# Sixteen-head attention and windowed transformer kernel: one eviction moved from ScalarE to VectorE, and the planner's times of the windowed stage replaced

## The chip, the cores and the metric

One Trainium2 chip, one of its cores. The metric is the device time of one execution in microseconds (us); three executions of the kernel before gave 5361.24 to 5370.43 us, median 5363.51 us.

## The reference

Input x is 4 sequences of 1024 tokens with 128 features, fp32. Four residual parts follow each other, each on a normalised x:

```python
x = x + L0_attn(layernorm(x))     # A: 16 heads of 8, rotary, full softmax attention
x = x + L0_ffn(layernorm(x))      # B: 6 layers of windowed attention (16 heads of 64, window 32,
                                  #    l2-normalised rotary q and k) and a gated feed-forward net
x = x + L1_attn(layernorm(x))     # C: 16 heads of 8, rotary, causal attention
x = x + L1_ffn(layernorm(x))      # D: 4-head attention with shared k and v, then 8 experts, top 2
```

The part A and part C core, for each batch and head:

```python
scores = einsum('bhqd,bhkd->bhqk', q, k) / sqrt(8)
out = einsum('bhqk,bhkd->bhqd', softmax(scores), v) @ wo.T
```

## The kernel before

The four stages run one after the other with a meeting of all engines between them. In each stage one list of steps is made on the host (`order`), and each engine walks through the list and issues only its own part of every step. So the list fixes, engine by engine, a strict order; engines wait for each other by semaphores. A bank of PSUM has a pair of counters, filled and emptied.

**Stages A and C** (`mha_stage`) work on 16 units, each a batch and four heads, in slots. In a slot TensorE makes two score tiles of 128 queries x 512 keys ("first", L457), from which VectorE takes the row maxima (L638), and two score tiles of the transposed kind ("second", L473), of which ScalarE makes the exponentials (L569). The "first" of a unit run while the "second" of the unit before run. "first" has a ring of three banks (0 to 2), "second" and the transposes share a ring of four (3 to 6). Every two slots "values" (L486, eight matmuls) multiplies the exponentials by v and adds into bank 7; after eight of these (stage A; four or eight in the causal stage C) a chunk of 512 queries is done. The step "finish" then copies bank 7 to the tile ot (L577), so that the next chunk's "values" may begin, and "turn_back" transposes ot (L495) for VectorE to divide by the sums (L662, L669). "finish" sorts ahead of the "first" steps of its slot. There are 32 "finish" steps in each of the two stages. Once per batch, VectorE also does the layer norm of the batch to come, in three bursts ("norm").

**Stage B** (`local_stage`) handles 192 tiles (6 layers, 4 batches, 8 tiles of 128 tokens) as a software pipeline planned by `local_order`. Tile i has a due time for each step: PERIOD (15.8) times i plus the time in PIECES; the feed-forward steps of a batch take three places per period at the times in FF_PIECES ("fill" for TensorE, "empty" for the engine that reads the bank). The events are sorted by time; nothing but their order reaches the chip. Norm steps of a batch (20 small ones, L1221, L1224 and after) and "apply" steps (8, L1202) have fixed times of their own, and fall in one period of eight each. The steps of a tile, with their lines: "project" (L986, banks 0 and 1), "square" (ScalarE, L1133), "rope" (VectorE, L1263 and L1267), "sum_squares" (L1275), "add" (GpSimd, L1407, L1409), "invert" (ScalarE square root L1137, VectorE L1281, L1283), "scale" (GpSimd, L1416), "turn" (TensorE, L994, banks 2 and 3), "copy_turned" (ScalarE, L1149), "score" (L1009, L1030, banks 4 and 5), "top" (L1292), "less" (L1301), "exp" (ScalarE, L1155), "sum" (L1307), "invert_sum" (L1312), "weigh" (GpSimd, L1423), "block" (VectorE transpose, L1320), "gather" (L1047, banks 4 to 7), "spread" (ScalarE, L1163), "out" (L1062), "join" (L1329). The feed-forward steps use bank 6; their "empty" on VectorE is L1355 (0.70 us) or L1363 (0.25 us).

The lines that place a step:

```python
    def put(period, time, *step):
        events.append((PERIOD * period + time, len(events), step))
    ...
    for i, (l, b, t) in enumerate(stream):
        for kind, times in PIECES.items():
            for c, time in enumerate(times):
                put(i, time, kind, i, c)
    ...
    return [step for _, _, step in sorted(events)], stream, number
```

Of the kernel before, what the change touches and what calls it, by code (L numbers as in the profile page):

```python
# [23 lines left out]
BANK = 512  # L24
# [278 lines left out]
def mha_stage(chip, name, w_names, biases, rot, causal):  # L303
    nc, ins, x, ident, banks = chip.nc, chip.ins, chip.x, chip.ident, chip.banks
    filled, emptied = chip.filled, chip.emptied
    dim, scale = 8, float(1.0 / np.sqrt(np.float32(8)))
# [3 lines left out]
    number, slot = chip.place(order, dict(  # L310
        first=cycle((0, 1, 2)), **{kind: singles for kind in ("second", "weights", "turn_x", "project", "turn_k", "turn_q1",
                                                           "turn_q2", "turn_back", "turn_o", "conclude")}))
# [5 lines left out]
    end_of_values = {step[1:3]: step for step in order if step[0] == "values"}  # L318
# [3 lines left out]
    with ExitStack() as scope:  # L322
# [8 lines left out]
        top = sb("top", [TILES, HEADS_PER_UNIT])  # L331
# [184 lines left out]
        def scalar_():  # L516
            e, q = nc.scalar, chip.scalar
            for step in order:
# [43 lines left out]
                if kind == "second":  # L562
# [4 lines left out]
                    if j >= PROBS:  # L567
                        q.wait_ge(sem["valued"], number["values", *seconds[j - PROBS][1:4]])
                    e.activation(prob[j % PROBS][:, lo:BANK], banks[n][:, lo:BANK], ACT.Exp,  # L569
                                 scale=scale).then_inc(emptied[n], 1)  # L570
                if kind == "finish":
                    c = step[2]
                    q.wait_ge(sem["valued"], number[end_of_values[i, c]])
                    if i:
                        at, turned = slot["turn_back", i - 1, c]
                        q.wait_ge(filled[at], turned)
                    e.copy(ot[:, BANK * c:BANK * (c + 1)], banks[7]).then_inc(sem["finished"], 1)  # L577
                if kind == "turn_o":
                    c = step[2]
                    q.wait_ge(filled[n], use)  # L580
# [5 lines left out]
        def vector_():  # L586
# [22 lines left out]
            for step in order:  # L609
# [30 lines left out]
                if kind == "shift":  # L640
                    mine = slice(4 * (i % 4), 4 * (i % 4) + 4)
                    high, low = (qx[i // 4 % 2][:, :, mine, 3 * dim + m] for m in range(2))
                    for back in range(3):
                        at, reduced = slot[firsts[number[end_of_first[i]] - 1 - back]]
                        q.wait_ge(emptied[at], reduced)
                    q.wait_ge(sem["zeroed"], i // 4)
                    e.tensor_reduce(top[:, :, :], top2[i % 2][:, :, :, :].rearrange("p t c g -> p t g c"), AX.X, ALU.max,
                                    negate=True).then_inc(*chain.step())
                    q.wait_ge(*chain.now())
                    at, turned = slot["turn_q1", i, CHUNKS - 1]  # L650
                    q.wait_ge(filled[at], turned)
                    e.tensor_copy(high, top[:, :, :]).then_inc(*chain.step())
                    q.wait_ge(*chain.now())
                    e.tensor_tensor(low, top[:, :, :], high.bitcast(F32), ALU.subtract).then_inc(sem["shifted"], 1)
                if kind == "turn_back":
                    c = step[2]
                    of_heads = banks[n].rearrange("p (t g w) -> p t g w", t=TPB, g=HEADS_PER_UNIT)
                    q.wait_ge(filled[n], use)
                    if number[step] > 1:
                        at, evicted = slot[("turn_back", i, 0) if c else ("turn_back", i - 1, CHUNKS - 1)]  # L660
                        q.wait_ge(emptied[at], evicted)
                    e.reciprocal(rsum[:, :, :], of_heads[:, :, :, dim]).then_inc(*chain.step())  # L662
                    q.wait_ge(*chain.now())
                    if i >= 4:
                        at, turned = slot["turn_o", i // 4 - 1, CHUNKS - 1]
                        q.wait_ge(filled[at], turned)
                    to = o[:, TPB * c:TPB * (c + 1), (i % 4) * 32:(i % 4 + 1) * 32].rearrange(
                        "p t (g d) -> p t g d", g=HEADS_PER_UNIT)
                    e.tensor_tensor(to, of_heads[:, :, :, 0:dim], bcast(rsum[:, :, :], 3, dim),  # L669
                                    ALU.mult).then_inc(emptied[n], 1)  # L670
# [79 lines left out]
NORM_BEGINS, NORM_STEP, APPLY_BEGINS, APPLY_STEP, BIAS_BEGINS = 2.0, 0.55, 2.0, 0.6, 6.0  # L750
MOVE_X, PLACE_X, MOVE_F, PLACE_F, SHIFT_CUT = 5.0, 12.0, 7.0, 16.5, 112
PIECES = dict(
    project=(0.29, 2.26, 8.62, 12.22), square=(3.47, 8.24, 10.89, 13.29), rope=(4.23, 10.44, 11.24, 15.80),
    sum_squares=(9.15, 11.10, 12.42, 15.72), add=(12.15, 16.43, 18.41, 19.63), invert=(14.25, 15.94, 16.10),
    scale=(18.56, 19.37, 19.62, 27.79), turn=(18.81, 20.62, 23.32, 29.42), copy_turned=(20.83, 23.54, 26.19, 30.02),
    score=(30.62, 32.29), top=(34.55, 34.71), less=(35.28, 35.71), exp=(35.59, 36.09),
    sum=(36.29, 36.51), invert_sum=(36.39, 37.10), weigh=(36.53, 37.46), block=(37.59, 39.49),
    gather=(43.67,), spread=(42.51, 42.52, 43.74, 47.20), out=(49.64, 51.29, 52.13, 52.87), join=(54.63,))
INVERT_PARTS = len(PIECES["invert"])
NORM_ROOT = 2 * TILES + 1  # L760
FF_PIECES = dict(fill=(15.99, 20.10, 24.25), empty=(17.52, 21.35, 24.51))
def local_order():


# [1400 lines left out]
```

## Time and profile before

| | |
|---|---|
| median of three runs | 5363.51 us (5361.24 to 5370.43) |
| the profiled execution | 5370.43 us, span 5369.1 us |
| TensorE / VectorE / ScalarE / GpSimd busy | 92% / 82% / 68% / 54% |
| stage A, about | 60 to 850 us |
| stage B, about | 900 to 3980 us |
| stage C, about | 4100 to 4700 us |
| stage D, about | 4760 to 5369 us |

The profile is of one execution, the slowest of the three, so its time stands 6.9 us above the median. A busy share of TensorE counts from the start of a matmul to its modelled end, so that neighbouring matmuls overlap in it. The column PEclk is the granted TensorE clock, 1.00 for 2.4 GHz and 0.50 for 1.2 GHz. In a timeline a row joins like instructions that follow each other; in brackets stands the idle time of the engine before it and the engine, tile and line that ended it.

### The profile page before, as it was taken

The page shows a single profiled execution, that of the slowest core. Times are in us where ns is not written, and L with a number is a line of the kernel's source. Part 1 is how long each engine was busy: PE and PEld are TensorE (multiplying, and loading weights), DVE is VectorE, ACT ScalarE, POOL GpSimd, SP SyncE. Part 2 cuts the span into 40 slices and gives each one's busy share as a digit, 9 for nine tenths or more (in the row PEclk, how much of TensorE's full clock was granted, in tenths as well). Part 3 has the DMA queues.
Part 4 walks back from the last instruction along what each step waited for, and adds up shares of the span by engine and source line. Part 5 has one row for each costly group of instructions (what it writes and reads, how often), then busy time and mean ns, then how long its engine had stood idle before and what let it go on. Part 6 is the DMA issues. An engine that isn't in the chain of part 4 may idle for free. (4 is left out here: it accounts for less than half of the span.)

```text
span 5369.1 us, 142691 instructions
## 1 busy us (share of the span) xinstructions
PE 4948.3 (92%) x59480; PEld 2999.0 (56%) x59480; DVE 4396.4 (82%) x9191; ACT 3628.2 (68%) x6463; POOL 2880.2 (54%) x3367
## 2 busy tenths in 40 slices
PE   6999997999999999999999999999986999978978
PEld 2333333666666666666666666666654555544445
DVE  7998995988898888989898989899945777567665
ACT  2888885777777777777777777777742777645522
POOL 2121003878777877787778777877731111024624
PEclk6999998999999999999999999999985999888989
DMA  0000002000000000000000000000000000000000
GB/s 23 1 1 1 1 1 71 14 10 10 26 14 10 10 25 14 10 10 26 14 10 10 27 16 12 10 10 14 4 3 24 2 2 2 2 15 1 1 1 16
DMA packets 46742, 63.25 MB, mean 12 GB/s; under 512 B 11261, under 2 KB 33603, under 8 KB 45203
## 3 DMA queue, kind: packets, MB, share of 16 engines
q1 hardware_dynamic: 46098, 54.14, 3.4%
q8 instruction: 469, 7.68, 0.6%
q14 instruction: 175, 1.43, 0.1%
HBM read 25.17 MB, written 4.19 MB: 5 GB/s over the span
## 5 line engine op out<-in xcount | busy, mean ns | idle before, releaser
L1062 PE MATMUL psum<-b_w_vo,b_mixed 128*128 128x128 f32 x6144 | 828.1, 278 | 3.4 <-ACT b_mixed L1163 3.2
L986 PE MATMUL psum<-b_w_qk,b_xst 128*128 128x512 f32 x1536 | 810.1, 609 | 9.2 <-DVE b_cross L1267 8.1
L1416 POOL TENSOR_TENSOR x<-x,b_norm 128x512 f32<-128x512 f32 x576 | 588.3, 1042 | 374.8 <-DVE b_norm L1283 374.8
L1062 PEld LDWEIGHTS psum<-b_w_vo,b_mixed 128*128 128x128 f32 x6144 | 751.9, 192 | 66.9 <-issue 50.0
L638 DVE TENSOR_REDUCE a_top<-psum 128x1 f32<-128x512 f32 x1024 | 637.4, 682 | 77.7 <-PE psum L457 75.8
L569 ACT ACTIVATE a_prob<-psum 128x512 f32<-128x512 f32 x1024 | 557.0, 606 | 117.7 <-PE psum L473 107.5
L1133 ACT ACTIVATE x<-psum 128x512 f32<-128x512 f32 x768 | 465.3, 606 | 204.6 <-DVE b_norm L1275 191.4
L1163 ACT COPY b_mixed<-psum 128x512 f32<-128x512 f32 x768 | 411.0, 587 | 230.7 <-PE psum L1047 230.7
L1275 DVE TENSOR_REDUCE b_norm<-x 128x8 f32<-128x512 f32 x768 | 513.9, 672 | 61.6 <-ACT x L1133 58.6
L1267 DVE TENSOR_TENSOR b_cross<-psum,b_table 128x512 f32<-128x512 f32 x768 | 521.3, 679 | 0.0
L638 DVE TENSOR_REDUCE c_top<-psum 128x1 f32<-128x512 f32 (+3 forms) x768 | 383.5, 551 | 151.9 <-PE psum L457 149.2
L1407 POOL TENSOR_TENSOR x<-x,b_cross 128x256 f32<-128x256 f32 x576 | 418.6, 727 | 147.5 <-DVE b_cross L1267 146.2
L1423 POOL TENSOR_TENSOR b_prob<-b_prob,b_stat 128x512 f32<-128x512 f32 x384 | 394.7, 1049 | 130.0 <-DVE b_stat L1312 126.3
L569 ACT ACTIVATE c_prob<-psum 128x512 f32<-128x512 f32 (+3 forms) x768 | 334.9, 501 | 152.7 <-PE psum L473 148.4
L1409 POOL TENSOR_TENSOR x<-x,b_cross 128x256 f32<-128x256 f32 x576 | 419.4, 728 | 0.0
L457 PE MATMUL psum<-a_kt,a_q 32*128 32x512 f32 x1024 | 358.7, 528 | 63.2 <-DVE a_top L638 57.3
L1263 DVE TENSOR_TENSOR x<-psum,b_table 128x512 f32<-128x512 f32 x576 | 390.8, 678 | 18.5 <-ACT x L1133 17.7
L1030 PEld LDWEIGHTS psum<-b_k_t,b_q_t 64*32 64x32 f32 x26368 | 308.2, 105 | 161.9 <-issue 131.1
L986 PEld LDWEIGHTS psum<-b_w_qk,b_xst 128*128 128x128 f32 x1536 | 246.6, 191 | 250.5 <-DVE b_cross L1267 138.3
L457 PEld LDWEIGHTS psum<-a_kt,a_q 32*128 32x128 f32 x1024 | 148.3, 193 | 389.7 <-DVE a_top L638 308.7
L994 PEld LDWEIGHTS psum<-ident,x 128*128 128x128 f32 x2304 | 278.2, 141 | 156.8 <-issue 132.2
L1030 PE MATMUL psum<-b_k_t,b_q_t 64*32 64x64 f32 (+1 forms) x26368 | 346.1, 220 | 2.9 <-issue 2.7
(326 smaller groups left out, 11042.7 us busy)
## 6 DMA issues: line engine op xcount, KB each, us to landing
b_prev<-b_xs_x SPq DMA_DIRECT2D x24, 384.0 KB, 3.5
b_w_qk<-in_L_ffn_Wqkv SPq DMA_DIRECT2D x6, 1024.0 KB, 7.1
b_shifted_x<-y SPq DMA_DIRECT2D x24, 224.0 KB, 2.5
b_shifted_f<-y SPq DMA_DIRECT2D x24, 224.0 KB, 2.5
b_w_v<-in_L_ffn_Wqkv SPq DMA_DIRECT2D x6, 512.0 KB, 7.4
b_w_o<-in_L_ffn_Wo SPq DMA_DIRECT2D x6, 512.0 KB, 9.2
b_prev<-b_xs_x SPq DMA_DIRECT2D x24, 112.0 KB, 3.3
x<-in_L_attn_x SPq DMA_DIRECT2D x4, 512.0 KB, 6.8
```

The lines of the kernel that those rows point to most:

```text
L457: e.matmul(banks[n][:, 0:wide], q1[i % 2][part, P * t:P * (t + 1)], kt[i % 3][part, BANK * c:hi], start=not corner, stop=True, skip_group_ ...
L569: e.activation(prob[j % PROBS][:, lo:BANK], banks[n][:, lo:BANK], ACT.Exp, scale=scale).then_inc(emptied[n], 1)
L638: e.tensor_reduce(top2[i % 2][:, t, c, head:head + 1], banks[n][:, 0:wide], AX.X, ALU.max).then_inc(emptied[n], 1)
L986: e.matmul(banks[n], xst_of(l, b)[:, P * t:P * (t + 1)], w_qk[l % 2][:, BANK * c:BANK * (c + 1)], start=True, stop=True).then_inc(filled[n ...
L1030: made = e.matmul(heads[rows, p, to, :], qt[half, p, rows], k[:, lo:lo + wide].rearrange("p (s q) -> p s q", q=WINDOW), start=False, stop= ...
L1062: made = e.matmul(banks[n][:, 0:D], mixed[:, h, :], w_vo[l % 2][:, h, :], start=h == 0, stop=h == 2 * PAIRS - 1)
L1133: e.activation(square[r % 2], banks[n], ACT.Square).then_inc(sem["squared"], 1)
L1267: e.tensor_tensor(by_head(cross[(nth[step] - 1) % 3]), by_head(banks[n]), bcast(table[:, t, k + 1, :], 1, HPC), ALU.mult).then_inc(emptied ...
L1275: e.tensor_reduce(norm[i % 2][:, 0, HPC * c:HPC * (c + 1)], by_head(square[r % 2]), AX.X, ALU.add).then_inc(sem["summed"], 1)
L1407: e.tensor_tensor(rh[:, :, 0:half], rh[:, :, 0:half], xh[:, :, half:LDIM], ALU.subtract).then_inc(*chain.step())
L1409: e.tensor_tensor(rh[:, :, half:LDIM], rh[:, :, half:LDIM], xh[:, :, 0:half], ALU.add).then_inc(sem["roped"], 1)
L1416: e.tensor_tensor(rh, rh, bcast(norm[i % 2][:, 1, HPC * c:HPC * (c + 1)], 2, LDIM), ALU.mult).then_inc(sem["scaled"], 1)
```

## The change

In stages A and C the copy of "finish" moves from ScalarE's walk through the list to VectorE's; its waits and its place in the list stay. In stage B all of PIECES but "rope" 0 and 1 and some further single values, and FF_PIECES, get other numbers. PERIOD, the norm, apply, move and place times stay.

```diff
@@ scalar_() of mha_stage
-                if kind == "finish":
-                    c = step[2]
-                    q.wait_ge(sem["valued"], number[end_of_values[i, c]])
-                    if i:
-                        at, turned = slot["turn_back", i - 1, c]
-                        q.wait_ge(filled[at], turned)
-                    e.copy(ot[:, BANK * c:BANK * (c + 1)], banks[7]).then_inc(sem["finished"], 1)
@@ vector_() of mha_stage
+                if kind == "finish":
+                    c = step[2]
+                    q.wait_ge(sem["valued"], number[end_of_values[i, c]])
+                    if i:
+                        at, turned = slot["turn_back", i - 1, c]
+                        q.wait_ge(filled[at], turned)
+                    e.tensor_copy(ot[:, BANK * c:BANK * (c + 1)], banks[7]).then_inc(sem["finished"], 1)
@@ PIECES
-    project=(0.29, 2.26, 8.62, 12.22), square=(3.47, 8.24, 10.89, 13.29), rope=(4.23, 10.44, 11.24, 15.80),
-    sum_squares=(9.15, 11.10, 12.42, 15.72), add=(12.15, 16.43, 18.41, 19.63), invert=(14.25, 15.94, 16.10),
-    scale=(18.56, 19.37, 19.62, 27.79), turn=(18.81, 20.62, 23.32, 29.42), copy_turned=(20.83, 23.54, 26.19, 30.02),
-    score=(30.62, 32.29), top=(34.55, 34.71), less=(35.28, 35.71), exp=(35.59, 36.09),
-    sum=(36.29, 36.51), invert_sum=(36.39, 37.10), weigh=(36.53, 37.46), block=(37.59, 39.49),
-    gather=(43.67,), spread=(42.51, 42.52, 43.74, 47.20), out=(49.64, 51.29, 52.13, 52.87), join=(54.63,))
+    project=(-0.02, 2.74, 8.92, 11.78), square=(2.41, 7.84, 10.76, 12.81), rope=(4.23, 10.44, 11.41, 15.62),
+    sum_squares=(9.27, 11.10, 12.03, 15.20), add=(12.65, 13.99, 17.94, 20.17), invert=(14.94, 17.16, 17.32),
+    scale=(19.10, 19.10, 20.57, 26.31), turn=(18.96, 22.74, 24.33, 29.08), copy_turned=(20.83, 22.40, 26.53, 30.10),
+    score=(30.19, 33.37), top=(33.89, 34.97), less=(34.99, 35.74), exp=(34.06, 36.34),
+    sum=(36.07, 36.88), invert_sum=(36.27, 36.99), weigh=(36.51, 36.91), block=(37.82, 40.61),
+    gather=(42.91,), spread=(42.72, 42.49, 43.36, 47.43), out=(49.27, 50.84, 52.64, 53.00), join=(56.06,))
-FF_PIECES = dict(fill=(15.99, 20.10, 24.25), empty=(17.52, 21.35, 24.51))
+FF_PIECES = dict(fill=(14.63, 20.66, 24.59), empty=(16.52, 21.90, 24.93))
```

## Rows read from the trace of the kernel before

**Rows 1.** The page: busy time and share of the span, by engine.
```profile
PE 4948.3 (92%) x59480; PEld 2999.0 (56%) x59480; DVE 4396.4 (82%) x9191; ACT 3628.2 (68%) x6463; POOL 2880.2 (54%) x3367
```

**Rows 2.** Busy time by stretch: stretch and length, engines, PEclk, DMA share, GB/s.
```profile
60.00:850.00 790.00, 728.37 (x4739) 277.33 (x4738) 666.87 (x1220) 618.91 (x1186) 97.66 (x54) 0.93 0.00 1
...
900.00:3900.00 3000.00, 2910.37 (x42974) 1970.37 (x42974) 2700.41 (x5483) 2242.39 (x3714) 2344.54 (x2913) 1.00 0.05 14
...
4100.00:4700.00 600.00, 574.02 (x7583) 317.72 (x7582) 415.87 (x951) 402.47 (x910) 70.38 (x48) 0.89 0.01 2
```

**Rows 3.** The same view, three stretches of stage A, the last two with a norm.
```profile
148.00:257.00 109.00, 100.42 (x711) 37.20 (x711) 101.61 (x181) 92.86 (x178) 8.75 (x6) 1.00 0.00 1
257.00:289.00 32.00, 28.81 (x171) 11.07 (x167) 27.54 (x69) 22.13 (x44) 0.00 (x0) 0.84 0.00 1
...
445.00:479.00 34.00, 32.59 (x168) 11.62 (x164) 27.55 (x69) 22.07 (x44) 0.00 (x0) 0.70 0.01 1
```

**Rows 4.** Line L577: min/median/max ns, first and last start; who waited for it.
```profile
L577 ACT COPY a_ot<-psum x32: 585/603/647, 147.0 to 845.7; 128x512 f32<-128x512 f32 x32
...
  PEld psum L486: 3.3, 13
```

**Rows 5.** Line L1334 of stage B: VectorE's copies of a full bank.
```profile
L1334 DVE COPY b_w_v<-psum x12: 652/684/692, 878.8 to 3105.4; 128x512 f32<-128x512 f32 x12
```

**Rows 6.** Waits of stage A, 60 to 850 us: waiter <- releaser: us, times, longest.
```profile
DVE a_rsum L662 <- PE psum L495: 42.3, 3, 16.5
```

**Rows 7.** Timeline of stage A around one "finish" (start, us, engine, line).
```profile
613.67 0.63 ACT L577 COPY a_ot<-psum 128x512 f32<-128x512 f32 x1
...
613.91 2.48 DVE L638 TENSOR_REDUCE a_top<-psum 128x1 f32<-128x512 f32 x4 [0.23 <-PE psum L457]
...
614.65 0.50 PE L457 MATMUL psum<-a_kt,a_q 32*128 32x512 f32 x1 [0.43 <-DVE a_top L638]
...
616.09 0.50 PE L457 MATMUL psum<-a_kt,a_q 32*128 32x512 f32 x2
...
616.62 1.29 DVE L638 TENSOR_REDUCE a_top<-psum 128x1 f32<-128x512 f32 x2 [0.23 <-PE psum L457]
```

**Rows 8.** Timeline of stage C around one "finish".
```profile
4192.48 3.38 DVE L638 TENSOR_REDUCE c_top<-psum 128x1 f32<-128x256 f32 x6 [0.46 <-PE psum L457]
...
4194.13 0.49 PE L457 MATMUL psum<-c_kt,c_q 32*128 32x512 f32 x1 [0.34 <-DVE c_top L638]
...
4196.18 1.02 DVE L638 TENSOR_REDUCE c_top<-psum 128x1 f32<-128x384 f32 x2 [0.31 <-PE psum L457]
```

**Rows 9.** Waits in stage B, 1000 to 3900 us.
```profile
POOL b_prob L1423 <- DVE b_stat L1312: 114.6, 120, 2.8
...
PEld psum L1047 <- DVE b_prob_t L1320: 113.1, 107, 1.8
...
DVE b_prob_t L1320 <- POOL b_prob L1423: 61.6, 138, 1.3
```

**Rows 10.** Timeline of a period of stage B with "apply" steps.
```profile
2343.15 1.26 ACT L1202 ACTIVATE b_xs_f<-b_xs_f,spread 128x128 f32<-128x128 f32 x3
...
2344.14 0.23 DVE L1363 TENSOR_TENSOR y<-y,psum 128x128 f32<-128x128 f32 x1
...
2346.31 1.04 POOL L1416 TENSOR_TENSOR b_rot<-b_rot,b_norm 128x512 f32<-128x512 f32 x1
...
2346.59 0.63 ACT L1155 ACTIVATE b_prob<-b_prob 128x512 f32<-128x512 f32 x1
...
2347.52 0.61 ACT L1155 ACTIVATE b_prob<-b_prob 128x512 f32<-128x512 f32 x1
...
2350.11 0.60 PE L994 MATMUL psum<-ident,b_rot 128*128 128x128 f32 x4
...
2350.89 0.71 DVE L1320 STREAM_TRANSPOSE b_prob_t<-b_prob 128x512 f32<-128x512 f32 x1 [1.17 <-POOL b_prob L1423]
```

**Rows 11.** Timeline of a period of stage B with norm steps, VectorE.
```profile
2335.61 0.21 DVE L1224 BATCH_NORM_AGGREGATE mean_var<-moments 128x2 f32<-128x6 f32 x2
```

## The prediction

> **What bounds the kernel now.** The page comes first: TensorE is busy for 92% of the span, VectorE for 82% [rows 1], so two engines are near their limit and the stages have to be read one by one. The view by stretches [rows 2] gives, of each 100 us: stage A 92 on TensorE and 84 on VectorE, stage B 97 and 90, stage C 96 and 69. ScalarE has 22 to 33% to spare in all three. In the steady part of stage A VectorE is busy for 93% [rows 3].
>
> The timeline shows what holds stage A [rows 7]. A round is two slots: four row maxima on VectorE, 2.48 us together and 0.60 us from one start to the next, then 0.23 us in which it waits for TensorE, and the round comes again after 2.71 us (613.91 to 616.62). It is a circle. The first maximum of a round frees a bank, for which the fourth "first" matmul waits (0.43 us at 614.65); behind it in TensorE's order stand two "second" matmuls and the eight "values" matmuls, which end about 616.09, then come the next "first" and the next maximum. So what makes the first maximum of a round late by some time makes everything late by that time. ScalarE's copy L577 isn't in the circle: the weight loads behind it waited 3.3 us in 13 cases of both stages [rows 4], and the round that holds a copy (613.67) takes the usual 2.71 us.
>
> In stage C VectorE has room on the average, but not at the end of a chunk [rows 8]: six maxima follow without a gap, and TensorE waits for the third of its banks at 4194.13. In stage B TensorE is the bound, with one wait that comes back in most tiles: the gather's weights wait for VectorE's transpose L1320, 113.1 us in 107 cases [rows 9]. It closes the circle of a tile: scores, top, less, exp, sum, weigh, block, gather, spread, and the next scores in the banks that spread has freed.
>
> **Part 1: the copy in stage A.** ScalarE loses 32 copies of 0.603 us [rows 4]; that gains nothing, since nobody waits for it. VectorE gets 32. It has no such copy in this stage; the nearest row is its copy of a full bank in stage B, 0.684 us [rows 5], and by the maxima such a thing takes 0.60 us of the engine from start to start [rows 7]. "finish" stands in VectorE's list ahead of the "first" of its slot, so the copy lands just where VectorE waits 0.23 us. The "values" it waits for have ended by then (ScalarE could start at 613.67, the four maxima before end there too). The first maximum starts 0.60 - 0.23 = 0.37 us later, the fourth "first" waits 0.80 us instead of 0.43, and nothing in the round takes that back. Three copies at the end lie where VectorE waits for TensorE anyway, 42.3 us in 3 cases [rows 6], and cost nothing. Two lie in the bursts of norms, where VectorE has no gap: 0.60 us each. Sum: 27 x 0.37 + 2 x 0.60 = 11.2 us. Bounds: 0, if TensorE made it up from the idle time of its own, and 29 x 0.68 = 20 us.
>
> VectorE sits farther from PSUM than ScalarE: the Trainium skill (Perfetto Trace Analysis, Optimizing Scalar/DVE Operations) gives about 125 ns of access overhead for the one and 51 ns for the other, and advises to offload a saturated VectorE to ScalarE, the reverse of this edit. The rows agree on the size, 0.684 against 0.603 us [rows 4, 5]; 74 ns on 64 copies would be an estimated 5 us of engine time.
>
> **Part 2: the copy in stage C.** 32 copies again, three of them in the tail. At a chunk end like that of [rows 8] the copy delays the maxima by 0.60 us, TensorE's wait of 0.34 us grows by it, and TensorE, 96% busy, has nothing to catch up with. At the other chunk ends the bank is only just free in time. I take 0.35 us, between nothing and 0.60: 29 x 0.35 = 10.2 us; bounds 0 and 29 x 0.68 = 20 us.
>
> **Part 3: the planned times.** Only the order counts, so I sort the times modulo 15.8 with both sets. In a usual tile just four things change places; the times move by up to 3 us, but mostly in company.
> - TensorE: "out" group 3 now runs before "turn" 1 (all but the first tiles). The turned piece is copied by ScalarE one such group later; ScalarE is 75% busy [rows 2], and the scores that need it are due 11 later in the new times (turn 1 22.74, score 1 33.37). 0.
> - ScalarE: "spread" 1 before "spread" 0. The four parts of a gather run side by side on four row groups of the array and end together. 0.
> - GpSimd: "add" 3 before "scale" 2, so scale 2 ends 1.5 us later. In [rows 10] it ends at 2347.35 and turn 2 starts at 2350.11: covered by 1.3 us. 0.
> - VectorE: the first "empty" of a period before the two "invert" steps, where VectorE does it (89 tiles: 44 of 0.23 us like that at 2344.14 [rows 10], 45 of 0.70). The inverse comes later by this, and so does scale 0 on GpSimd. GpSimd waits ahead of "weigh" in 120 tiles [rows 9], there it is swallowed. Taking 23 tiles (the "apply" ones, where GpSimd runs from scale to weigh without a stop) at 0.2 us: +4.6 us. Bounds 0 and 89 x 0.25 = 22 us.
>
> Two periods in eight also see the small steps, whose times stay, in another place. In the 23 "apply" periods exp 0 now goes ahead of four of the eight apply steps, which then stand between exp 0 and exp 1. Exp 0 can start earlier than the 2346.59 of [rows 10] by the apply step it passes, 0.4 us; four apply steps at 0.42 us (1.26 us for three) bring exp 1 to about 2348.5, 1.0 us later than 2347.52. VectorE's sum 1 waits for some 0.4 us, and block 0, which now waits 1.17 us for weigh, takes most of it: +0.1 us, 2.3 us in all; bounds -0.4 x 23 = -9 and +1.0 x 23 = 23 us. In the 23 norm periods two aggregations more go ahead of block 1, 0.2 us [rows 11]; but top 0, less 0 and the first sum each pass a norm step of about that size. I set these against each other, -0.1 us each, -2.3 us; bounds -6 and +5. Stage B: 4.6 + 2.3 - 2.3 = 4.6 us, rounded to +4, since a few of these overlap.
>
> **Sum.** 11.2 + 10.2 + 4 = 25.4 us. On the profiled execution's own 5370.4 us that makes 5395.8; the median of the runs shown is 6.9 us lower, so I say 5388.9, rounded to 5389 us.
>
> **The rivals.**
> - *The new order shortens the circle of stage B.* The place is the wait of gather for block. If scale, add and weigh on GpSimd mesh better and the softmax chain starts earlier, and that takes 0.35 us from each of the 107 waits of about 1.06 us [rows 9], then 37 us go: 5389 - 4 - 37 = 5348, faster than before. It decides once it is worth more than 32 us, 0.17 us for each of the 192 tiles. For it: that all tiles share this circle. Against it: the steps in the circle keep their places in the usual tile; only 46 periods see a change in it.
> - *The copies are hidden.* If the gap of VectorE and TensorE's own spare time take in the copies in both stages, only stage B's 4 us stay: 5368 us, no change. For it: VectorE's 31% of idle time in stage C. Against it: the circle of [rows 7], with 0.23 us of room.
> - *The clock falls more often.* In the two norm stretches of stage A the granted clock is 0.84 and 0.70 of 2.4 GHz [rows 3], that is 10 and 20 us at 1.2 GHz; VectorE's work is the same (27.54 and 27.55 us), the stretch is 2 us longer, so 10 us of the lower clock cost 2 us. A copy within each burst makes TensorE pause longer. Should six batch changes of A and C each lose 10 us more of full clock, that is 12 us: 5401 us. What the Trainium skill says (TensorE: Matmul & The Clock Gate, What's actually happening), that idleness brings the lower clock back and activity lifts it, agrees with these rows.
>
> **How the numbers follow.** Forecast 0.52, shorter circle 0.14, copies hidden 0.16, clock 0.12, others (stage B slower by more than its price, towards 5410) 0.06. Within 0.2% means 10.7 us on either side of 5363.5, about what a measurement of this kernel can tell from no change. Faster: the shorter circle and a little of the others, 0.15. Same: the hidden copies and the low end of the forecast, 0.20. Slower: 0.65. The forecast's own bounds, 5374 to 5402, come from the copies at half and at full price. The range leaves out the far half of the shorter circle and the worst of stage B: 5352 to 5404 us.
>
> **What the new profile would show.** Step 1: L577's work as a VectorE copy of 0.65 to 0.70 us; the round with a copy 3.08 us instead of 2.71; 148 to 812 us of stage A longer by about 10 us; ScalarE's busy time lower by 39 us and VectorE's higher by 44. Step 2: in stage C a longer wait of TensorE for the maxima L638. Step 3: stage B, first project to last, the same within 10 us, with the gather's wait for L1320 near its 113 us. The prediction is wrong if stage B moves by more than 20 us either way, which I can't exclude by a sorted list alone, or if rounds with a copy stay at 2.71 us.

## The result and the profile after

The changed kernel takes 5413.6 us (median of 5 runs, 5405.5 to 5421.6), the kernel before in the same series 5370.4 us. The ratio is 1.0079, with a 95% interval of 1.0058 to 1.0099: 43 us slower. The forecast was 5389 us with a range up to 5404; the sign was right, the size was not. The profiled execution after took 5425.4 us, with a span of 5424.1 us.

Busy time in the page of the changed kernel, which answers to [rows 1]:

```profile
PE 4975.2 (92%) x59480; PEld 3004.8 (55%) x59480; DVE 4434.1 (82%) x9255; ACT 3599.4 (66%) x6399; POOL 2883.1 (53%) x3367
```

VectorE has 64 instructions and 37.7 us more, ScalarE 64 fewer and 28.8 us less. These numbers say that the copies moved; they say nothing of where 43 us went. The same three stretches as in [rows 2] (stretch and length, busy time of PE, PEld, DVE, ACT, POOL, PEclk, DMA share, GB/s):

```profile
60.00:850.00 790.00, 721.80 (x4675) 273.31 (x4679) 682.13 (x1249) 600.65 (x1142) 97.58 (x54) 0.92 0.00 1
900.00:3900.00 3000.00, 2891.32 (x42486) 1949.79 (x42487) 2679.97 (x5445) 2213.60 (x3672) 2322.09 (x2885) 1.00 0.05 14
4100.00:4700.00 600.00, 560.43 (x7205) 315.75 (x7203) 434.76 (x988) 371.06 (x820) 74.18 (x50) 0.87 0.01 2
```

In the 3000 us of stage B all engines have done less: 42,486 matmuls instead of 42,974, at a granted clock of 1.00 in both. So stage B, in which nothing but an order changed, has become slower too. To compare stages I measure them in each trace between two marks of their own: A and C from the first to the last "turn_back" (L495) of the stage, B from the first matmul of "out" of its first tile to that of its last (191 tile periods).

| | A | B | C |
|---|---|---|---|
| before | 696.4 | 3037.3 | 545.4 |
| after | 706.9 | 3058.8 | 563.4 |
| difference | +10.5 | +21.5 | +18.0 |
| forecast | +11.2 | +4 | +10.2 |

The rest of the 55 us between the two profiled executions lies in the first and last tiles of B (2.5 us), in D (2.8 us, from its first matmul to the end) and between the stages. The largest error is in stage B. The waits of the forecast's circle there, 1000 to 3900 us, as in [rows 9]:

```profile
POOL b_prob L1423 <- DVE b_stat L1312: 98.6, 108, 2.6
...
PEld psum L1047 <- DVE b_prob_t L1320: 117.9, 110, 2.0
...
DVE b_prob_t L1320 <- POOL b_prob L1423: 62.2, 132, 1.4
```

The gather's wait has grown by 4.8 us and GpSimd's has shrunk by 16. The circle has neither shortened nor become the place of the loss. By the measure that the forecast named for stage B, first "project" to last, it is 23.3 us longer.

### The profile page after: what moved, and what is told of

The parts are those of the page before. It is cut to its first block and busy times, and to the rows that moved or that the text cites. A ratio compares the mean times of both kernels' runs of the same rounds, so it can differ in the third digit from the quotient of the medians.

```text
span 5424.1 us, 142815 instructions
## 1 busy us (share of the span) xinstructions
PE 4975.2 (92%) x59480; PEld 3004.8 (55%) x59480; DVE 4434.1 (82%) x9255; ACT 3599.4 (66%) x6399; POOL 2883.1 (53%) x3367
## 3 DMA queue, kind: packets, MB, share of 16 engines
q14 instruction: 176, 1.44, 0.1%
## 5 line engine op out<-in xcount | busy, mean ns | idle before, releaser
L986 PE MATMUL psum<-b_w_qk,b_xst 128*128 128x512 f32 x1536 | 811.4, 610 | 7.6 <-DVE b_cross L1267 6.4
L1062 PE MATMUL psum<-b_w_vo,b_mixed 128*128 128x128 f32 x6144 | 797.1, 278 | 3.2 <-ACT b_mixed L1163 2.9
L1062 PEld LDWEIGHTS psum<-b_w_vo,b_mixed 128*128 128x128 f32 x6144 | 736.9, 192 | 67.3 <-issue 50.6
L1030 PEld LDWEIGHTS psum<-b_k_t,b_q_t 64*32 64x32 f32 x26368 | 308.8, 105 | 172.5 <-issue 141.9
L1149 ACT COPY b_q_t<-psum 128x512 f32<-128x512 f32 x384 | 220.5, 574 | 263.5 <-PE psum L994 263.5
L986 PEld LDWEIGHTS psum<-b_w_qk,b_xst 128*128 128x128 f32 x1536 | 247.2, 191 | 249.6 <-DVE b_cross L1267 134.8
```

Of the source, the lines that this page charges most:

```text
L986: e.matmul(banks[n], xst_of(l, b)[:, P * t:P * (t + 1)], w_qk[l % 2][:, BANK * c:BANK * (c + 1)], start=True, stop=True).then_inc(filled[n ...
L1062: made = e.matmul(banks[n][:, 0:D], mixed[:, h, :], w_vo[l % 2][:, h, :], start=h == 0, stop=h == 2 * PAIRS - 1)
```

## The experiments

Each kernel below is the kernel before or after with one edit. A "pause" is a gap of more than 0.1 us between the starts of two neighbouring matmuls of one score burst (L1030, 26,368 matmuls in stage B); it is counted in the trace. Stage lengths and pauses are those of one profiled execution, medians and ratios those of 4 to 12 runs against 21 to 31 runs of the kernel before (for the changed kernel 5 against 5).

| kernel | median us | ratio (95%) | A | B | C | pauses, us |
|---|---|---|---|---|---|---|
| before | 5370.4 | | 696.4 | 3037.3 | 545.4 | 13, 5.2 |
| after | 5413.6 | 1.0079 (1.0058 to 1.0099) | 706.9 | 3058.8 | 563.4 | 34, 17.5 |
| e1 copy only | 5388.8 | 1.0035 (1.0019 to 1.0051) | 706.9 | 3037.8 | 555.2 | 12, 5.6 |
| e2 times only | 5388.3 | 1.0034 (1.0023 to 1.0045) | 698.0 | 3059.5 | 538.6 | 33, 17.3 |
| e3 out 3, turn 1 | 5368.1 | 0.9997 (0.9984 to 1.0009) | 698.0 | 3043.4 | 556.6 | 14, 8.6 |
| e4 empty, invert | 5371.1 | 1.0001 (0.9988 to 1.0013) | 698.8 | 3040.5 | 538.6 | 19, 7.4 |
| e5 apply places | 5372.5 | 0.9995 (0.9980 to 1.0011) | 698.1 | 3038.9 | 557.2 | 14, 6.6 |
| e6 norm places | 5369.7 | 0.9997 (0.9984 to 1.0009) | 697.9 | 3042.3 | 538.6 | 13, 6.0 |
| e7 add 3 and spread 1 | 5382.5 | 1.0029 (1.0013 to 1.0045) | 698.7 | 3054.2 | 535.2 | 35, 19.6 |
| e8 table later | 5362.2 | 0.9990 (0.9975 to 1.0006) | 698.1 | 3035.4 | 556.7 | 16, 7.8 |
| e9 add 3 only | 5375.3 | 1.0004 (0.9995 to 1.0014) | 697.8 | 3037.7 | 542.2 | 14, 6.5 |
| e10 spread 1 only | 5387.9 | 1.0027 (1.0016 to 1.0039) | 697.8 | 3049.7 | 548.8 | 33, 13.7 |
| e11 after, both back | 5404.5 | 1.0062 (1.0049 to 1.0075) | 703.6 | 3046.6 | 561.0 | 9, 6.8 |
| e12 table later, again | 5361.0 | 0.9984 (0.9976 to 0.9993) | 698.7 | 3034.3 | 545.5 | 16, 7.2 |
| e13 spread 1 and masks | 5374.1 | 1.0015 (1.0003 to 1.0026) | 698.2 | 3043.3 | 538.7 | 12, 6.8 |
| e14 masks only | 5371.4 | 1.0002 (0.9991 to 1.0014) | 698.1 | 3043.7 | 548.9 | 26, 12.0 |
| e15 after and masks | 5412.4 | 1.0086 (1.0066 to 1.0106) | 704.0 | 3049.2 | 559.0 | 13, 6.0 |
| e16 copy twice | 5537.8 | 1.0335 (1.0307 to 1.0363) | 767.7 | 3038.2 | 631.4 | 12, 5.3 |

Stage B repeats well: before, e1 and e16, which have the same order there, lie within 0.9 us. Stage C does not: with the same code it is 535 to 557 us long in 13 of these profiles. Differences of B can be read from single profiles, those of C only from several.

Time and granted clock go together: over the 110 executions of the kernel before, 0.001 of the mean clock goes with 3.5 us (correlation -0.93). Take the 244 executions of e1 to e15 and of the kernel before that ran beside them to equal clock by a straight line, each within its own series. Then the kernels stand above the kernel before by an estimated 14.8 us (e1), 20.0 (e2), 1.0 (e3), 2.6 (e4), 0.8 (e5), 3.2 (e6), 14.6 (e7), -7.3 (e8), 1.8 (e9), 12.4 (e10), 24.0 (e11), -4.5 (e12), 5.7 (e13), 7.0 (e14) and 27.1 (e15), each +-2 us, e11 and e15 +-3; the changed kernel, by the same line, about 34. What an edit costs by way of a lower clock isn't in these numbers. They bear out the lengths of B from single profiles, with one exception: e3, +6.1 us in its profile and 1.0 here.

**e1 and e2, the two halves of the change.**

```diff
 e1: "finish" in vector_() as after; PIECES and FF_PIECES as before
 e2: "finish" in scalar_() as before; PIECES and FF_PIECES as after
```

> The copy on VectorE alone, all planned times as before. Theory 1 (the copy sits in the circle of stages A and C): first to last transpose of the chunks in stage A longer by 10 to 11 us, in stage C by about 9 us plus what a stretch at the lower clock adds, stage B's 3037.3 us from the first to the last tile's first out group unchanged; time about 20 us above before. Theory 2 (the cost of the whole change lies in stage B only, C's 18 us were a chance stretch of the lower clock): about 11 us above before, C within 5 us.

> The new planned times alone, the copy on ScalarE as before. Theory 1 (the new order costs stage B about 21 us by fixed waits): stage B longer by 20 to 23 us, A and C as before, time 20 to 25 us above before. Theory 2 (pauses inside TensorE's score matmuls, 17 us in the profile after against 5 us before, are chance of one execution): stage B longer by some 10 us only.

The halves give 18.4 and 17.9 us of medians, 36 of the 43 us, and the intervals leave room for the rest; at equal clock they are 14.8 and 20.0 of about 34. In both, the first theory came true. The copy lengthens A and C and leaves B alone, the times lengthen B and leave A and C alone. The pauses came again in e2, 33 of them, so they are no chance of one execution.

**e3 to e7, the new order in parts.** Together their order changes are those of the new times, and no more.

```diff
 e3
-turn=(18.81, 20.62,
+turn=(18.81, 21.30,
 e4
-invert=(14.25, 15.94, 16.10)
+invert=(14.25, 17.60, 17.62)
 e5
-square=(3.47,
+square=(2.41,
-exp=(35.59, 36.09)
+exp=(34.06, 36.34)
 e6
-top=(34.55, 34.71), less=(35.28, 35.71)
+top=(33.89, 34.97), less=(34.99, 35.74)
-sum=(36.29, 36.51), invert_sum=(36.39, 37.10)
+sum=(36.07, 36.88), invert_sum=(36.27, 36.99)
-block=(37.59, 39.49), join=(54.63,), sum_squares=(9.15,
+block=(37.82, 40.61), join=(56.06,), sum_squares=(9.27,
-empty=(17.52, 21.35, 24.51)
+empty=(17.52, 21.90, 24.93)
 e7
-add=(12.15, 16.43, 18.41, 19.63), spread=(42.51, 42.52,
+add=(12.15, 16.43, 18.41, 19.50), spread=(42.51, 42.50,
```

> Before, with one place changed: out group 3 ahead of turn 1 on TensorE in 190 tiles. Theory 1 (the loss is in waits on GpSimd and ScalarE): stage B within 3 us of 3037.3, pauses inside the score matmuls near 5 us. Theory 2 (this swap brings the pauses inside the score matmuls): stage B 10 to 12 us longer, with pauses of about 17 us.

> Before, with one place changed: the first empty of a period ahead of the inverts on VectorE in 89 tiles. Theory 1 (scale 0 starts later, and where table steps keep GpSimd busy until weigh the delay goes through to the gather): stage B 5 to 8 us longer, most of it in the fourth batch of each layer, about 0.45 us in a tile with an empty of 0.65 us. Theory 2 (GpSimd's idle time ahead of weigh swallows it): within 2 us.

> Before, with square 0 and exp 0 ahead of the apply steps on ScalarE as in the change (23 tiles). Theory 1 (exp 1 comes 0.8 to 1 us later and VectorE's block waits): stage B 3 to 6 us longer, in the apply tiles. Theory 2 (block's wait for weigh swallows it): within 1 us.

> Before, with the steps of VectorE placed among the norm steps as in the change (23 tiles). Theory 1 (two aggregations ahead of block 1 delay the gather, nothing gives it back): stage B 3 to 4 us longer, in the norm tiles. Theory 2 (top, less and the first sum come earlier and pay for it): within 1 us or shorter.

> Before, with add 3 ahead of scale 2 on GpSimd and spread 1 ahead of spread 0 on ScalarE in all 192 tiles. Theory 1 (both are covered): stage B within 2 us of 3037.3. Theory 2 (the irregular losses of up to 0.6 us in single tiles come from scale 2 arriving late at turn 2, or from the spreads): 5 us or more longer.

Only e7 moves the median. Of the 22.2 us that e2 adds to stage B, e7 alone gives 16.9. The other four give 6.1, 3.2, 1.6 and 5.0 us in B, each below what their medians can tell from nothing; together with e7 that is more than e2, so they overlap. In e7 the second theory came true. The 5.0 us of e6 are above both of its theories and nearer to the first; e3, e4 and e5 lie between their two theories and decide nothing.

**e8 and e12, a side path.** Not part of the change: GpSimd's table steps are planned 1.9 us later.

```diff
-            put(i, max(PIECES["add"]) + 0.5, "table", l + 1, t)
+            put(i, max(PIECES["add"]) + 2.4, "table", l + 1, t)
```

> Not a part of the change: before, with the table steps (GpSimd, four operations of 0.33 us, 40 tiles) placed behind weigh 1 instead of ahead of weigh 0. Theory 1 (in the fourth batch of a layer GpSimd's chain from scale to weigh is what block waits for): stage B 10 to 20 us shorter, in those 40 tiles. Theory 2 (another wait takes its place at once): within 4 us.

> The kernel before with GpSimd's table steps planned 1.9 us later in the tile, as run once before in fewer rounds (5362.2 us against 5370.8, ratio 0.999 with an interval of 0.9975 to 1.0006). If the steps stood in the way of add and scale in the eight tiles of the table, the gain is some 2 us in stage B (3035.4 against 3037.3) and the ratio stays within 0.2% of 1: nothing that can be told from no change. Rival: the 8 us seen are real, ratio 0.9985 with an interval below 1.

The second series puts it 8.7 us under the kernel before, with an interval of 0.9976 to 0.9993. Stage B is 1.9 and 3.0 us shorter, so the gain of 10 to 20 us there, the first theory of e8, did not come. Of all kernels here it is the fastest, by 0.16%, which is real by its interval but less than the 0.2% named in the prediction, and where the rest of the 8.7 us comes from stays open.

**e9 and e10, e7 taken apart.**

```diff
 e9
-add=(12.15, 16.43, 18.41, 19.63)
+add=(12.15, 16.43, 18.41, 19.50)
 e10
-spread=(42.51, 42.52,
+spread=(42.51, 42.50,
```

> The kernel before with one swap only: GpSimd's add 3 ahead of its scale 2 (planned time of add 3 from 19.63 to 19.50). Together with the swap of spread 1 and spread 0 it lengthened stage B (first to last tile of out 0) by 16.9 us (3054.2 against 3037.3) and the time by 12 us, with 35 pauses of over 0.1 us inside the score matmuls, 19.6 us together, where the kernel before has 13 and 5.2 us. Theory add: GpSimd's order sets when the instruction blocks of TensorE are fetched; this kernel alone shows stage B at 3054 +-4 us, 30 or more pauses, a median near 5382 us. Theory spread: ScalarE's order does it; then stage B is 3037 to 3042 us here, 12 to 19 pauses, 5370 us. Theory both: about 3046 us.

> The kernel before with one swap only: ScalarE's spread 1 ahead of its spread 0 (planned time of spread 1 from 42.52 to 42.50). Theory add: nothing comes of it, stage B 3037 to 3042 us, 12 to 19 pauses in the scores, 5370 us. Theory spread: stage B 3054 +-4 us, 30 or more pauses, 5382 us. Theory that any small shift of the schedule reshuffles the pauses by chance: both halves differ from the kernel before, and the two do not add up to 16.9 us.

It is the swap on ScalarE: B +12.4 us with "spread" 1 first, +0.4 with "add" 3 first. (The two add up to 12.8, e7 had 16.9 in its one profile. At equal clock they are 1.8 and 12.4 us, e7 14.6, so nothing is left over that the executions show.) What happens is seen in tile 146, which starts at 3258.89 us in the kernel before and at 3271.46 in e10. The timeline of the kernel before, TensorE and ScalarE:

```profile
3268.75 0.30 PEld L986 LDWEIGHTS psum<-b_w_qk,b_xst 128*128 128x128 f32 x2 [0.76 <-DVE b_cross L1267]
...
3268.81 1.56 ACT L1163 COPY b_mixed<-psum 128x512 f32<-128x512 f32 x3 [1.21 <-PE psum L1047]
...
3272.69 0.86 PE L1030 MATMUL psum<-b_k_t,b_q_t 64*32 64x64 f32 x64
...
3273.48 0.71 PE L1062 MATMUL psum<-b_w_vo,b_mixed 128*128 128x128 f32 x4
```

And that of e10:

```profile
3281.23 0.30 PEld L986 LDWEIGHTS psum<-b_w_qk,b_xst 128*128 128x128 f32 x2 [0.76 <-DVE b_cross L1267]
...
3281.34 1.56 ACT L1163 COPY b_mixed<-psum 128x512 f32<-128x512 f32 x3 [1.24 <-PE psum L1047]
...
3285.17 0.43 PE L1030 MATMUL psum<-b_k_t,b_q_t 64*32 64x64 f32 x25
...
3286.13 0.64 PE L1030 MATMUL psum<-b_k_t,b_q_t 64*32 64x64 f32 x39 [0.53 <-issue]
...
3286.70 1.16 PE L1062 MATMUL psum<-b_w_vo,b_mixed 128*128 128x128 f32 x8
```

Two things are to be seen. The three copies begin 0.11 us after L986's weights, not 0.06: the part that is now copied first is ready later, by 0.04 us in the median of the tiles. And score 1, one burst of 64 matmuls before, breaks off after 25 and goes on 0.53 us later. No engine is named as the releaser, only "issue": TensorE had no instructions. All 33 pauses of e10 lie, to within four matmuls, a whole number of blocks of 126.5 matmuls apart. Such a block is one packet of 16,384 bytes on the DMA queue of kind "instruction": there are 469 packets for the 118,960 weight loads and matmuls and 1,266 semaphore instructions, 256 for each packet. In tile 146 the packet that matters starts 10.28 us after the tile's start in the kernel before and at 12.12 in e10, and takes 1.3 us; until then TensorE's rows agree to 0.01 us. The pause ends at 14.78, 1.4 us after the packet is in.

The same holds of every pause. In the 17 kernels of the table without e16 there are 326 pauses. Ahead of each of them the last instruction packet is the one that belongs to this place of the program, counted from the start, and the pause ends 1.2 to 1.7 us after this packet is in. So the pauses are waits for instructions, and they begin where a packet comes too late for the burst.

The Trainium skill (Runtime: NRT & Kernel Launch, Instruction fetch mechanics) describes just such blocks of 16 KiB that the sequencer fetches by itself while it executes the one before, and holds the cost of a boundary to be mostly hidden. The trace of the kernel before agrees in the main, with 13 pauses and 5.2 us; in e10 (33 pauses, 13.7 us) and in the changed kernel (34, 17.5 us) much less of it is hidden.

**e11, the two swaps undone in the changed kernel.**

```diff
-add=(12.65, 13.99, 17.94, 20.17), spread=(42.72, 42.49,
+add=(12.65, 13.99, 17.94, 20.60), spread=(42.48, 42.49,
-            put(i, max(PIECES["add"]) + 0.5, "table", l + 1, t)
+            put(i, max(PIECES["add"]) + 0.07, "table", l + 1, t)
```

> The changed kernel with these two swaps undone (scale 2 ahead of add 3, spread 0 ahead of spread 1; the table steps stay in their place), all other new orders and the copy on VectorE kept. If the two swaps carry the loss of stage B in the changed kernel as they do alone, stage B comes to 3040 to 3048 us instead of 3058.8, the pauses in the scores to about 7 us instead of 17.5, and the median to 5413.6 - 15 = about 5399 us, with ratio 1.005. Rival: the pauses belong to the sum of the new orders, and undoing two of them leaves stage B at 3055 to 3060 us and the median at 5410 to 5415 us.

Stage B gets 12.2 us shorter and the pauses go down to 9. The ratio to the kernel before falls from 1.0079 to 1.0062; the two intervals overlap, so the stage says it more surely than the time. At equal clock it is 24.0 us instead of about 34.

**e13 to e15, why a swap on ScalarE starves TensorE.** The scores of the next tile go into banks 4 and 5, which "spread" 0 and 1 empty. Ahead of score 0 TensorE makes its masks (L1009), four into bank 4 and four into bank 5, each four behind a wait for their bank. These kernels turn that order round.

```diff
-                    for odd in range(2 if step[2] == 0 else 0):
+                    for odd in ((1, 0) if step[2] == 0 else ()):
```

> The kernel before with spread 1 ahead of spread 0 on ScalarE (which alone gave stage B 3049.7 us instead of 3037.3 and 33 pauses inside the score matmuls, 13.7 us together) and with TensorE's masks for score 0 taking bank 5 ahead of bank 4 too. Theory late release: TensorE's sequencer stands at the wait for bank 4 ahead of the masks; with spread 1 first, bank 4 is copied 0.48 us later, the sequencer runs through the block of instructions 0.5 us later, the next block is fetched 0.5 us later, and score 1 catches up with it. Taking bank 5 first gives the lead back: stage B 3037 to 3040 us, 12 to 19 pauses of 5 to 8 us, median 5370 us. Rival, the order on ScalarE itself (its copies start 0.04 us later in each tile): stage B stays at 3048 to 3051 us with 30 or more pauses, median 5387 us.

> The mirror of it: the kernel before, spread 0 first as it was, but the masks for score 0 take bank 5 ahead of bank 4. Theory late release: TensorE now waits first for the bank that is copied second, so this costs what the swap of the spreads costs: stage B 3048 to 3052 us, 30 or more pauses of 13 us or more, median about 5385 us. Rival, the order on ScalarE itself: nothing changes, 3037 to 3040 us, 5370 us.

> The changed kernel with one more edit: the masks for score 0 take bank 5, which its spread 1 now frees first, ahead of bank 4. Theory late release: as with the two swaps undone (stage B 3046.6 us instead of 3058.8, 9 pauses of 6.9 us): stage B 3045 to 3049 us, median about 5402 us, ratio 1.006. Rival: 3057 to 3060 us and 5412 us.

The four kernels make a square:

| | masks: bank 4 first | masks: bank 5 first |
|---|---|---|
| spread 0 copied first | before: 3037.3 us, 13 pauses | e14: 3043.7 us, 26 pauses |
| spread 1 copied first | e10: 3049.7 us, 33 pauses | e13: 3043.3 us, 12 pauses |

Wherever TensorE first asks for the bank that is copied second, the pauses double; where both orders agree, they are as few as in the kernel before, whichever bank leads. The trace shows each step between. TensorE's sequencer records the wait ahead of the masks as an instruction of its own. It ends 0.7 us after the start of the first copy in 160 of 190 tiles in the kernel before, e13 and e15, and 1.2 us after it in the same number in e10, e14 and the changed kernel: one copy later. In the other 30 another wait comes first. Behind it the sequencer runs on through its program, ahead of the array (in tile 146 of the kernel before the wait ends 0.76 us before the first mask), and with it the fetching. Of 79 packets that the kernel before requests between 11.3 and 13.5 us of a tile, those that come over 0.3 us later are 35 in e10 and 32 in e14, but 7 in e13, and 9 in e1 and in e9; 41 in the changed kernel, 11 in e15. The waits of TensorE in the scores for "issue", 900 to 3900 us (total, times, longest), one fence each for the kernel before, e14, e10, e13, after and e15:

```profile
PE psum L1030 <- issue: 2.7, 3, 1.8
```

```profile
PE psum L1030 <- issue: 6.8, 12, 1.9
```

```profile
PE psum L1030 <- issue: 6.6, 14, 2.0
```

```profile
PE psum L1030 <- issue: 4.2, 2, 2.2
```

```profile
PE psum L1030 <- issue: 9.7, 23, 1.5
```

```profile
PE psum L1030 <- issue: 3.0, 5, 1.9
```

This is only the part that lies behind a row's last modelled end, but the times fall into the same two groups. The square also adds up: the mismatch alone costs 6.4 us (e14), the order of the copies alone 6.0 us (e13), both 12.4 (e10). My expectation for e13 and e14 missed this: I had put all 12.4 us on the mismatch. At equal clock it is 7.0 us for e14, 5.7 for e13 and 12.4 for e10, from 11 or 12 executions each, though the median of e14 shows nothing. Of the 6.0 us of e13, 3.5 lie in 64 periods that are 0.02 to 0.1 us longer, which fits copies that start 0.04 us later: the kernels with "spread" 1 first have 48 to 64 such periods, those with "spread" 0 first 7 to 15. The other 2.5 us are in larger, irregular differences, and neither part was tried by itself. In e15 stage B came down by 9.6 us, as expected, but the median of its four runs, 5412.4 us, did not; at equal clock it is 27.1 us instead of about 34.

**e16, the copy made twice.**

```diff
-                    e.tensor_copy(ot[:, BANK * c:BANK * (c + 1)], banks[7]).then_inc(sem["finished"], 1)
+                    e.tensor_copy(ot[:, BANK * c:BANK * (c + 1)], banks[7]).then_inc(*chain.step())
+                    q.wait_ge(*chain.now())
+                    e.tensor_copy(ot[:, BANK * c:BANK * (c + 1)], banks[7]).then_inc(sem["finished"], 1)
```

> The kernel before with the copy on VectorE, and made twice, the second after the end of the first (0.68 us and some 0.05 us of waiting). The same values are written twice. With one copy stage A grew by 10.5 us and stage C by 9.8 us. If the copy lies in a circle without room, as the prediction has it, all of the second copy is added: stage A 706.9 + 29 x 0.73 = 728 us, +-3; stage C 555 + up to 21 = 565 to 576 us; stage B stays at 3037.8; the median about 5388.8 + 40 = 5425 to 5430 us. Rival, a loss that comes from a changed order of events and not from VectorE's time: stage A stays below 715 us.

Against the kernel with one copy A grew by 60.8 us and C by 76.2, where 21 and at most 21 were expected; both theories missed it. In the chunks that go undisturbed the addition is as expected: 23.26 us instead of 22.54, +0.72. The others show another thing, here in a round of stage A of e16:

```profile
560.76 0.69 DVE L656 COPY a_ot<-psum 128x512 f32<-128x512 f32 x1
...
561.36 2.48 DVE L631 TENSOR_REDUCE a_top<-psum 128x1 f32<-128x512 f32 x4
562.10 0.79 PE L457 MATMUL psum<-a_kt,a_q 32*128 32x512 f32 x1 [1.44 <-DVE a_top L631]
...
565.52 1.29 DVE L631 TENSOR_REDUCE a_top<-psum 128x1 f32<-128x512 f32 x2 [1.68 <-PE psum L457]
```

TensorE stood still for 1.44 us, and its next "first" takes 0.79 us instead of 0.50: the granted clock has fallen to 1.2 GHz, and now VectorE waits 1.68 us for TensorE. Over 148 to 812 us the mean granted clock is 0.89 here and 0.98 in the kernel before. In stage A one copy per chunk costs its own time, and a second one costs the clock as well; in stage C the first one already does.

## Why the prediction was wrong, step by step

**What bounds the kernel** was read rightly for A and C. For B the bound was right (TensorE), but the list of what can stop it was not: it held waits for data and banks, not TensorE's own supply of instructions.

**Part 1, stage A: the mechanism was right, its size too high by half.** Against the kernel before it is 10.5 us after and in e1, with 11.2 predicted. But that profile of the kernel before happens to be the shortest in A. The 13 kernels with the old copy have a mean of 698.1 us there, and the four with the new one (706.9 twice, 703.6, 704.0) of 705.4: 7.3 us, with the same time at 1.2 GHz (35 and 36 us). VectorE's copy was given 0.65 to 0.70 us and measured:

```profile
L654 DVE COPY a_ot<-psum x32: 678/679/692, 147.3 to 856.6; 128x512 f32<-128x512 f32 x32
```

A round with the copy, in the timeline after, beside [rows 7]:

```profile
620.27 2.48 DVE L631 TENSOR_REDUCE a_top<-psum 128x1 f32<-128x512 f32 x4 [0.22 <-PE psum L457]
...
622.67 0.68 DVE L654 COPY a_ot<-psum 128x512 f32<-128x512 f32 x1
...
623.26 2.47 DVE L631 TENSOR_REDUCE a_top<-psum 128x1 f32<-128x512 f32 x4
624.00 0.49 PE L457 MATMUL psum<-a_kt,a_q 32*128 32x512 f32 x1 [0.70 <-DVE a_top L631]
...
625.97 1.29 DVE L631 TENSOR_REDUCE a_top<-psum 128x1 f32<-128x512 f32 x2 [0.23 <-PE psum L457]
```

The copy does land ahead of the first maximum, VectorE's wait is gone, and the fourth "first" waits longer. But it waits 0.70 us, not 0.80, and from 620.27 the next round begins after 2.99 us, not 3.08. The step was mis-sized: I subtracted the idle time of 0.23, which counts from the end of the last maximum, from a price of 0.60 that counts from start to start. From start to start four maxima take 2.40 of 2.71 us, so 0.31 us is free, and 0.60 - 0.31 = 0.29. The chunks without a norm grew by about 0.3 us each. Around the two bursts of norms, priced at 0.60 us each, the means of the four kernels are 1.2 us longer in the first and 0.1 us shorter in the second. The last three chunks, priced at nothing, took 0.5 us less. The busy times, forecast at 39 us less on ScalarE and 44 more on VectorE, came to 28.8 and 37.7. They count overlapping instructions once, so the price is again the one from start to start: 64 x 0.60 = 38 us on VectorE, and on ScalarE, where three copies take 1.56 us and so 0.48 each, 64 x 0.48 = 31.

**Part 2, stage C: the mechanism was right, but half of the cost is the clock's.** e1 had +9.8 us for the predicted 10.2. At an undisturbed chunk end like that of [rows 8], in e1, the same stretch takes 4.05 us instead of 3.70, the 0.35 us that I took:

```profile
4238.48 0.76 DVE L631 TENSOR_REDUCE c_top<-psum 128x1 f32<-128x256 f32 x2 [0.45 <-PE psum L457]
...
4242.53 1.02 DVE L631 TENSOR_REDUCE c_top<-psum 128x1 f32<-128x384 f32 x2 [0.31 <-PE psum L457]
```

The chunk end of [rows 8] itself went otherwise in e1. In the kernel before, TensorE's eight "values" behind the wait of 0.34 us take:

```profile
4194.56 1.07 PE L486 MATMUL psum<-c_prob,c_v 128*32 128x512 f32 x8
```

In e1:

```profile
4203.77 0.76 DVE L631 TENSOR_REDUCE c_top<-psum 128x1 f32<-128x256 f32 x2 [0.45 <-PE psum L457]
4204.44 0.68 DVE L654 COPY c_ot<-psum 128x512 f32<-128x512 f32 x1
4205.77 0.49 PE L457 MATMUL psum<-c_kt,c_q 32*128 32x512 f32 x1 [0.70 <-DVE c_top L631]
4206.21 1.93 PE L486 MATMUL psum<-c_prob,c_v 128*32 128x512 f32 x8
4209.06 1.02 DVE L631 TENSOR_REDUCE c_top<-psum 128x1 f32<-128x384 f32 x2 [1.55 <-PE psum L457]
```

TensorE waited 0.70 us instead of 0.34, then its granted clock fell to 1.2 GHz (for 3.4 us, from 4206.3), and the stretch took 5.29 us instead of 3.70. Away from the norm bursts and the tail, in chunks 0 to 3, 8 to 11 and 16 to 25, the four kernels with the new copy have 17 to 44 us at 1.2 GHz, the 13 with the old one 0 to 7.

Since single profiles scatter, I take means: 545.5 us over 13 kernels with the old copy, 559.7 over four with the new one, +14.1 us. In all of C the mean time at 1.2 GHz is 74 and 96 us, and over these 17 profiles each such us goes with 0.35 us of length. So an estimated 7.8 of the 14.1 us are the clock's and 6.4 the copy's own. This agrees with the undisturbed chunks, which grew by 0.27 to 0.35 us, while chunks 7, 15 and 23, the last of a batch, took 0.49 us less. That e1's single +9.8 met my 10.2 is luck: it is 6.4 us and some 3.6 us for 10 us more at 1.2 GHz than in the one profile before. The changed kernel had 31 us at 1.2 GHz from 4517 us on, and the two chunks there took 42.6 us instead of the 35.8 of e1.

**Part 3, stage B: wrong, +21.5 us for +4.** The step that failed is the one on ScalarE: "'spread' 1 before 'spread' 0. The four parts of a gather run side by side on four row groups of the array and end together. 0." The copies start 0.04 us later when "spread" 1 goes first, and, the larger error, I asked who waits for what the copies write and not for the banks that they free. This swap alone measured 12.4 us (e10), and to undo it together with the harmless "add" 3 took 12.2 us off the changed kernel (e11). What is left, 9.3 us, belongs to the other new orders: "out" 3 before "turn" 1, priced at 0, is +6.1 alone (1.0 +-2 at equal clock, so its size is open); the first "empty" before the inverts, priced at 4.6, is +3.2; apply periods, priced at 2.3, +1.6; norm periods, priced at -2.3, +5.0. The sum of the four single ones is 15.9, so they overlap, and the paths of e3 and e6 were not followed further. "Add" 3 before "scale" 2, priced at 0, is 0.4.

**The sum.** With the measured sizes it is 7.3 + 14.1 + 21.5 = 43 us, the 43 of the medians. The forecast had 11.2 + 10.2 + 4 = 25.4; stage B makes up 17.5 of the difference, and 7.3 + 6.4 for the copies' own time are less than the 21.4 that I gave them. (The forecast's own lower bound, 5374 us, is 5363.5 and the copies at half price without stage B's 4 us; with them it would be 5378.)

**The rivals.** The shorter circle did not come (the gather's wait is 117.9 us, not 76). The copies are not hidden (e1). The clock's rival, priced at 12 us, came true in part: 7.8 us in stage C, and not at the batch changes where I looked for them, but at chunk ends between them. In stage A it did not come. The first burst of [rows 3] has 0.68 in the changed kernel instead of 0.84:

```profile
257.00:289.00 32.00, 28.59 (x148) 10.36 (x147) 26.01 (x70) 18.38 (x36) 0.00 (x0) 0.68 0.00 1
```

But the same stretch in e9, which has the old copy, shows 0.68 too:

```profile
257.00:289.00 32.00, 30.30 (x158) 10.52 (x152) 26.53 (x71) 20.09 (x39) 0.00 (x0) 0.68 0.00 1
```

What came in the main was the case given 0.06, stage B slower by more than its price. The prediction named "stage B moves by more than 20 us" as what would refute it, and that is what happened.

## What to carry to other kernels

Two steps that "end together" and free two banks are not interchangeable: look up in which order their user asks for the banks, and keep both orders the same, for the wait that comes first holds up the whole queue behind it. When an engine with dense bursts of short instructions waits for "issue", compare the times of its instruction packets between the kernels; a wait that ends half a microsecond later ahead of the burst can reappear as a pause inside it. Before adding work to an engine in a tight round, count the room from start to start, not from the end of one row to the start of the next, and look in the profile after whether the longer waits of TensorE bring the lower clock.

## What the runs showed of the hardware

- TensorE can run out of instructions in the middle of a burst. A packet of 256 instructions took 1.1 us in the mean to arrive; a score burst, 64 matmuls with 64 weight loads, uses up half of one in 0.86 us. All 326 pauses of over 0.1 us in the score bursts of 17 kernels end 1.2 to 1.7 us after the packet of that place is in. e10 has TensorE's program of the kernel before, instruction by instruction, and yet 33 pauses of 13.7 us instead of 13 of 5.2: only the time of a wait ahead of the burst differs.
- TensorE's granted clock fell to 1.2 GHz after a standstill of 1.44 us in e16 (a "first" took 0.79 us instead of 0.50). After standstills of 0.70 us it fell at a chunk end of stage C in e1 (eight "values" took 1.93 us instead of 1.07) and not in the changed kernel's undisturbed rounds of stage A. In the measured stretch of stage C the time at 1.2 GHz differed between profiles of the same code from 44 to 106 us. Over 110 executions of the kernel before, the mean granted clock accounts for most of the scatter of its time (correlation -0.93).
